# Layer-1 keys and experts: turned rows kept by token chunk, fifteen early weight loads, a ring of twelve, down two experts behind

## The reference

```python
x = layernorm(x + L0_attention(x))          # memory banks, 16 heads
x = layernorm(x + L0_experts(x))            # 16 routed experts, 2 shared ones
x = layernorm(x + L1_attention(x))          # linear attention with a feature map of two layers
x = layernorm(x + L1_experts(x))

# L1_experts: E = 64 experts, K = 6 of them for each token, H = 512, F = 192, CAP = 96
scores = sigmoid(x @ gate_w)
topk_ids = grouped_topk(scores + bias, K)                # best 4 of 8 groups first
topk_w = 2.5 * normalised(scores at topk_ids)
buf = first CAP tokens that chose each expert            # [64, 96, 512]
h = silu(buf @ w_gate) * (buf @ w_up)                    # [64, 96, 192]
out = h @ w_down                                         # [64, 96, 512]
y = segment_sum(out * topk_w, token)
shared = silu(x @ ws_gate) * (x @ ws_up) @ ws_down
return y + shared
```

## Time and profile before

| quantity | value |
| --- | --- |
| device time, three runs | median 1588.38 us (1587.12 to 1590.78) |
| the profiled execution's own time | 1585.73 us |
| its span | 1583.9 us |
| mean granted TensorE clock | 0.926 |
| TensorE busy | 1347.1 us, 85% of the span |
| VectorE busy | 1078.5 us, 68% |
| ScalarE busy | 730.1 us, 46% |
| GpSimd busy | 759.9 us, 48% |
| moved by DMA | 212.68 MB, mean 134 GB/s |

### The profile page before, as it was taken

How to read it: one execution, slowest core, us unless ns; L and a number is a source line. 1 busy time by engine, 2 the same in 40 slices (tenths; PEclk the granted TensorE clock), 3 DMA queues, 4 the chain that set the end, 5 groups by cost and what they waited for, 6 DMA issues and landing times. The chain is left out here.

```text
span 1583.9 us, 21495 instructions
## 1 busy us (share of the span) xinstructions
PE 1347.1 (85%) x7253; PEld 1110.7 (70%) x7253; DVE 1078.5 (68%) x1795; ACT 730.1 (46%) x1158; POOL 759.9 (48%) x654
## 2 busy tenths in 40 slices
PE   5999859999599999946999789998897799999950
PEld 5787647767377777735899679987666577777740
DVE  5688757232388888865886556666395588888847
ACT  4121032000188888832454354444221588888840
POOL 1455520000388887833664323332274467777734
PEclk9899979999799999977999789999997899999985
DMA  4000040000366567632110000002422999999958
GB/s 167 1 1 27 27 134 2 1 0 0 132 222 212 175 186 251 234 120 54 49 54 2 10 28 1 1 1 100 155 86 108 334 338 338 341 340 339 336 145 318
DMA packets 81808, 212.68 MB, mean 134 GB/s; under 512 B 20426, under 2 KB 23498, under 8 KB 79292
## 3 DMA queue, kind: packets, MB, share of 16 engines
q1 hardware_dynamic: 50075, 133.14, 23.2%
q0 software_dynamic: 31120, 77.38, 17.4%
q10 hardware_dynamic: 528, 1.05, 0.2%
HBM read 208.75 MB, written 46.79 MB: 161 GB/s over the span
## 5 line engine op out<-in xcount | busy, mean ns | idle before, releaser
L66 PE MATMUL bank<-e_w_hi,e_xt_hi 128*96 128x384 f32 (+1 forms) x444 | 168.4, 379 | 3.1 <-DVE e_w_lo L2700 3.1
L68 PE MATMUL bank<-e_w_hi,e_xt_lo 128*96 128x384 f32 (+1 forms) x444 | 160.8, 362 | 0.0
L67 PE MATMUL bank<-e_w_lo,e_xt_hi 128*96 128x384 f32 (+1 forms) x444 | 160.7, 362 | 0.0
L1064 POOL DMA_INDIRECT e_w_raw<-in_w_gate_up,r_load_of x47 | 54.6, 1161 | 215.5 <-issue 215.5
L2590 POOL DMA_INDIRECT sums<-e_y,r_target_of x64 | 108.4, 1694 | 73.1 <-DMA sums<-e_y,r_target_of 41.6
L1189 DVE TENSOR_TENSOR e_w_lo<-e_w_raw,e_w_hi 128x2048 fp32r<-128x2048 f32 x47 | 107.7, 2292 | 33.9 <-ACT e_w_hi L1148 26.3
L2700 DVE TENSOR_TENSOR e_w_lo<-r_w_early,e_w_hi 128x1536 fp32r<-128x1536 f32 x48 | 84.8, 1767 | 25.9 <-ACT e_w_hi L2664 24.9
L231 POOL TENSOR_TENSOR a_read<-a_read_n 128x256 f32<-128x256 f32 x64 | 50.2, 785 | 103.7 <-DVE a_read_n L452 103.7
L1056 POOL DMA_INDIRECT e_xg<-rows,r_token_of x47 | 91.5, 1947 | 14.3 <-issue 14.3
L1757 POOL TENSOR_TENSOR q_g_lo<-q_gf,a_g 128x512 fp32r<-128x512 f32 x32 | 41.6, 1301 | 112.2 <-ACT a_g L1921 112.2
L1148 ACT ACTIVATE e_w_hi<-e_w_raw 128x2048 fp32r<-128x2048 f32 x47 | 89.8, 1910 | 0.0
(11 more groups left out here) (481 smaller groups left out, 4463.2 us busy)
## 6 DMA issues: line engine op xcount, KB each, us to landing
r_w_early<-in_w_gate_up SPq DMA_DIRECT2D x48, 768.0 KB
r_w_early<-in_w_down SPq DMA_DIRECT2D x24, 768.0 KB
results<-e_y SPq DMA_DIRECT2D x47, 256.0 KB
rows<-resid SPq DMA_DIRECT2D x8, 1024.0 KB, 4.4
r_w_first<-in_w_gate_up SPq DMA_DIRECT2D x8, 768.0 KB
r_low<-in_w_down SPq DMA_DIRECT2D x8, 768.0 KB
e_w_raw<-in_w_gate_up SPq DMA_DIRECT2D x8, 768.0 KB
resid<-in_x SPq DMA_DIRECT2D x4, 1024.0 KB, 5.5
```

What stands on the lines that cost most here:

```text
L66: pe.matmul(out, a_hi, b_hi, start=start, stop=False)
L67: pe.matmul(out, a_hi, b_lo, start=False, stop=False)
L68: return pe.matmul(out, a_lo, b_hi, start=False, stop=stop)
L1064: pool.indirect_dma_start(w1_raw[p][:, :], None, io["w_gate_up0"], bass.IndirectOffsetOnAxis(k.load_of[:, c:c + 1], 0), bounds_check=E0 * ...
```

## The change

The turned rows of layer-1 attention now lie in one tile `xt` of [128, 4 chunks, 2 halves, 4, 512], high and low of one chunk side by side; `TurnedRows` gives the two views. Their chunks come free one after the other while the shared expert runs, and weights of the first ten routed experts are loaded into them and into the residual rows `k.x` as soon as these are stored: ten of gate and up, five pairs of down. Two gate-up loads and one down load start ahead of the zero stores; the rest follows `s_gu` at 2, 4 and 6 and the landing of the residual stores of a chunk. `s_sums0` becomes one semaphore for each chunk. GpSimd gathers for three experts before the block ends. The shared-expert block waits for what it waited for before.

In the routed block the ring has U = 12 buffers of gate and up weights and 6 of pairs of down weights, with loads ten experts ahead, and NR = 6 buffers of gathered rows with the gather of g+5. `pipeline` replaces `three_stages` on TensorE, ScalarE and VectorE: each stage is given with its distance from g, in the order in which it runs. `silu` and `hidden` are cut in two (`down_hi`, `down_lo` hold the down weights' part). `turn_hidden(g-1)` comes behind `gate_up(g)`, `down` and `results` are two experts behind, and `add_results` is that of g-2.

In `attention1_keys` the order of calls changes: `tile(0)` moves up ahead of `combine(5)`, `keys(2)` ahead of `normalise(2)`, and `combine(6)` and `turn(4)` are written out ahead of the loop.

The diff, shortened:

```diff
+def pipeline(eng, n, unroll, *stages):
+
+    def step(g):
+        for stage, ahead in stages:
+            if 0 <= g + ahead < n:
+                stage((g + ahead) // unroll, (g + ahead) % unroll)
+
+    first, last = -max(ahead for _, ahead in stages), -min(ahead for _, ahead in stages)
+    rounds = (n + first - 1) // unroll
+    for g in range(first, 2 * unroll + 1):
+        step(g)
+    with eng.Fori(2, rounds) as i:
+        for q in range(unroll):
+            for stage, ahead in stages:
+                stage(i + (q + 1 + ahead) // unroll, (q + 1 + ahead) % unroll)
+    for g in range(unroll * rounds + 1, n + last):
...
+class TurnedRows:
+
+    def __init__(self, both, half):
+        self.both, self.half = both, half
+
+    def __call__(self, b, first, n):
+        c, at = first // CH, first % CH
+        return self.both[:, c, self.half, b, at:at + n]
...
-        xt = tuple(k.sb("a1_xt_" + n, [P, KD, T], F32R, ctx) for n in ("hi", "lo"))
+        both = sb("xt", [P, NC, 2, KD, CH], F32R)
+        xt = tuple(TurnedRows(both, half) for half in range(2))
...
             combine(4)
+            tile(0)
             combine(5)
             rstd(2)
+            keys(2)
             normalise(2)
-            for i in range(NT):
+            combine(6)
+            turn(4)
+            for i in range(1, NT):
                 if i + 6 < NT:
                     combine(i + 6)
                     if i % 2:
@@ -1327,11 +1361,9 @@
                     keys(i + 2)
                 if i % 2 and i + 6 < NT:
                     normalise((i + 5) // 2)
-                if i:
-                    before_tile(i - 1)
+                before_tile(i - 1)
                 tile(i)
-                if i:
-                    after_tile(i - 1)
+                after_tile(i - 1)
             before_tile(NT - 1)
             after_tile(NT - 1)
...
-    k.s_sums0, k.s_sums1 = k.sem("e1_first_sums_begun"), k.sem("e1_second_sums_begun")
+    k.s_sums0, k.s_sums1 = [k.sem(f"e1_first_sums_begun{c}") for c in range(NC)], k.sem("e1_second_sums_begun")
...
-    k.xg_low = [low[0:CAP, 3 * D + n * (D + E1):3 * D + (n + 1) * (D + E1)] for n in range(2)]
+    row_at = lambda a, o: a[0:CAP, o:o + D + E1]
...
-    k.w1_early = [k.w1_first] + [rt(f"w1_early{p}", [P, KD, 2 * F1]) for p in range(1, 7)]
-    k.w2_early = [rt(f"w2_early{q}", [P, 3, D]) for q in range(3)]
-    k.xg_early = [rt(f"xg_early{p}", [CAP, D + E1]) for p in range(4)]
-    rt("early_rest", [P, 2 * KD * T - 9 * KD * 2 * F1 - 4 * (D + E1)])
-    k.s_w1_early = [k.sem(f"e1_gate_up_loaded{p}") for p in range(7)]
-    k.s_w2_early = [k.sem(f"e1_down_loaded{q}") for q in range(3)]
-    k.s_xg_early = [k.sem(f"e1_rows_gathered{p}") for p in range(4)]
+    freed = rt("early", [P, NC * 2 * KD * CH])
+    UNIT = KD * 2 * F1
+    unit = lambda n: freed[:, n * UNIT:(n + 1) * UNIT]
+    resid = lambda n: k.x[:, 3 * n:3 * n + 3, :].rearrange("p i d -> p (i d)")
+    gate_up_of = lambda a: a.rearrange("p (b n) -> p b n", b=KD)
+    down_of = lambda a: a.rearrange("p (f n) -> p f n", f=3)
+    k.w1_early = [k.w1_first[:, :, :]] + [gate_up_of(a) for a in (unit(1), unit(2), unit(3), unit(5), unit(6), unit(8), unit(9), resid(1), resid(2))]
+    k.w2_early = [down_of(a) for a in (unit(0), unit(4), unit(7), resid(0), resid(3))]
+    k.xg_early = [row_at(freed, 10 * UNIT), row_at(low, 3 * D), row_at(low, 3 * D + D + E1)]
...
+                gate_up_early(0)
+                down_early(0)
+                gate_up_early(1)
...
+                sp.wait_ge(s_gu, 2)
+                gate_up_early(2)
+                gate_up_early(3)
+                down_early(1)
+                sp.wait_ge(k.s_rows, 2 * 16 * NC)
+                store_rows(0)
+                store_rows(1)
                 sp.wait_ge(s_share, 1)
                 sp.dma_start(k.rows1.rearrange("(i p) d -> p i d", p=P)[:, :, D:D + E1], share[:, :, :]).then_inc(s_shared, 16)
-                sp.wait_ge(k.s_rows, 2 * 16 * NC)
-                for c in range(NC - 1):
-                    sp.wait_ge(s_res, TC * (c + 1))
-                    sp.dma_start(k.sums[0][0:T, :].rearrange("(c j p) d -> c p j d", p=P, j=TC)[c],
-                                 k.x[:, c * TC:(c + 1) * TC, :]).then_inc(k.s_sums0, 16)
+                sp.wait_ge(s_gu, 4)
+                gate_up_early(4)
+                gate_up_early(5)
+                down_early(2)
+                sp.wait_ge(k.s_sums0[0], 16)
+                down_early(3)
+                sp.wait_ge(k.s_sums0[1], 16)
+                gate_up_early(8)
+                store_rows(2)
                 sp.wait_ge(s_gu, NU - 2)
-                for e in range(6):
-                    if e:
-                        sp.dma_start(k.w1_early[e][:, :, :].rearrange("p b n -> p (b n)"), io["w_gate_up"][e]).then_inc(k.s_w1_early[e], 16)
-                    if e % 2 == 0:
-                        sp.dma_start(k.w2_early[e // 2][:, :, :].rearrange("p f n -> p (f n)"), io["w_down"][e // 2]).then_inc(k.s_w2_early[e // 2], 16)
+                gate_up_early(6)
+                gate_up_early(7)
+                sp.wait_ge(k.s_sums0[2], 16)
+                gate_up_early(9)
+                down_early(4)
...
-                for e in range(4):
-                    pool.indirect_dma_start(k.xg_early[e][:, :], None, k.rows1, bass.IndirectOffsetOnAxis(k.token_of[:, e:e + 1], 0)
+                for e in range(3):
+                    pool.indirect_dma_start(k.xg_early[e], None, k.rows1, bass.IndirectOffsetOnAxis(k.token_of[:, e:e + 1], 0)
...
-        U, NX = 8, 4
+        U, NX, NR = 12, 4, 6
...
-                    if not past(h, p, 6):
+                    if not past(h, p, 10):
...
-                three_stages(sp, E1, nothing, nothing, nothing, ahead=load, unroll=U, lead=6)
+                three_stages(sp, E1, nothing, nothing, nothing, ahead=load, unroll=U, lead=10)
...
-                    if past(h, p, U):
+                    if e >= NR:
...
                         pool.wait_ge(s_g[p], gathered(h, p) - 16)
-                        pool.wait_ge(s_wt, e - U + 1)
+                        pool.wait_ge(s_wt, e - NR + 1)
...
-                for g in range(-2, E1 + 1):
-                    if g + 6 < E1:
-                        gather((g + 6) // U, (g + 6) % U)
-                    if g == 1:
-                        pool.wait_ge(k.s_sums0, 16 * NC)
+                for g in range(-2, E1 + 2):
+                    if g + 5 < E1:
+                        gather((g + 5) // U, (g + 5) % U)
+                    if g == 2:
+                        for c in range(NC):
+                            pool.wait_ge(k.s_sums0[c], 16)
                         pool.wait_ge(k.s_sums1, 16 * (NC + 2))
-                    if g >= 1:
-                        add_results((g - 1) // U, (g - 1) % U)
+                    if g >= 2:
+                        add_results((g - 2) // U, (g - 2) % U)
...
-                three_stages(pe, E1, turn, gate_up, down, between=turn_hidden, unroll=U)
+                pipeline(pe, E1, U, (turn, 1), (gate_up, 0), (turn_hidden, -1), (down, -2))
...
-                three_stages(act, E1, turned_hi, silu, results, between=hidden_hi, prepare=weights_hi, unroll=U)
+                pipeline(act, E1, U, (turned_hi, 1), (weights_hi, 1), (silu, 0), (hidden_hi, -1), (down_hi, 0), (results, -2))
...
-                three_stages(vec, E1, turned_lo, hidden, nothing, between=hidden_lo, prepare=weights_lo, unroll=U)
+                pipeline(vec, E1, U, (turned_lo, 1), (weights_lo, 1), (hidden, 0), (hidden_lo, -1), (down_lo, 0))
```

More of the change, by code:

```diff
@@ L1482, in turn @@
                     act.wait_ge(s_tps, n + 1)
-                    act.activation(xt_hi[:, 2 * half:2 * half + 2, c * CK:(c + 1) * CK], bank[0][:, :].rearrange("p (b t) -> p b t", b=2),
+                    act.activation(xt_hi(slice(2 * half, 2 * half + 2), c * CK, CK), bank[0][:, :].rearrange("p (b t) -> p b t", b=2),
                                    ACT.Copy).then_inc(s_thi, 1)
@@ L1550, in turn @@
                     vec.wait_ge(s_thi, n + 1)
-                    part = lambda a: a[:, 2 * half:2 * half + 2, c * CK:(c + 1) * CK]
+                    part = lambda a: a(slice(2 * half, 2 * half + 2), c * CK, CK)
                     vec.tensor_tensor(part(xt_lo), bank[0][:, :].rearrange("p (b t) -> p b t", b=2), part(xt_hi), ALU.subtract).then_inc(s_tlo, 1)
@@ L2518, in experts1_routed @@
     with ExitStack() as ctx:
-        U, NX = 8, 4
+        U, NX, NR = 12, 4, 6
         two = lambda name, shape, dt=F32: [k.sb(f"e1_{name}{p}", shape, dt, ctx) for p in range(2)] * (U // 2)
         four = lambda name, shape, dt=F32: [k.sb(f"e1_{name}{p}", shape, dt, ctx) for p in range(NX)] * (U // NX)
-        w1_raw = k.w1_early + [k.sb(f"e1_w1_raw{p}", [P, KD, 2 * F1], F32, ctx) for p in range(7, U)]
+        w1_raw = k.w1_early + [k.sb(f"e1_w1_raw{p}", [P, KD, 2 * F1], F32, ctx)[:, :, :] for p in range(10, U)]
```

(14 more changed lines are left out.)

46 lines of the change are left out of this document (26 added, 20 removed).

## The result

Fourteen executions of each kernel: before 1586.92 us median (1584.69 to 1591.04), changed 1581.94 us (1575.05 to 1591.24). The ratio is 0.996 with a 95% interval of 0.9947 to 0.9974. The change is faster, by about 5 us instead of the 19 forecast, and the executions scatter over 16 us where those of before scattered over 6. The profiled execution of the changed kernel took 1575.05 us, span 1573.3: it is the fastest of the fourteen, and what its profile says of a step has to be read with that in mind. Of the 10.6 us between the two profiled spans, 2.7 lie ahead of layer-1 keys (694.47 before, 691.81 now), in work that the change doesn't touch.

A forecast was written before the change was run, and what follows sets the result against it. DMA and TensorE looked full in the routed stage, with TensorE's own 4.23 us left as the step. Terms -3.5 - 5.5 - 10.7 - 0.5 + 1.0 = -19.2 gave 1566.5 profiled, 1569 median; 8-in-10 range 1560 to 1584.

The forecast's parts named there:

- the order inside a step: Routed experts of layer 1: moving turn_hidden behind gate_up shortens a step from 4.456 to 4.28 us, -10.7 us over 61 steps.
- The first rival: Routed stage: additions to the sums set the step, holding it near 4.44 us; 1575 to 1579 us, chance 0.20.
- Boundary: Between shared-expert and routed blocks: fewer loads and gathers left to drain, so the next block starts earlier, -5.5 us.
- Loads ahead of the stage: Shared-expert block: eleven loads moved ahead of 1218, where DMA was 0.34 busy, cost 0 us.
- Keys: Layer-1 keys: tile(0) ahead of combine(5) fills TensorE's gap ahead of turn(4), -3.5 us.
- Fifteen loads as a head start: Routed weights: 34.8 us of transfers loaded ahead cover 27.5 us of falling behind at 4.28 a step; no starving.
- Tail: End of the routed stage: down one step further behind lengthens the last chain, +1.0 us.
- Clock: First step of the routed block: shorter pause leaves the granted clock nearer to full, -0.5 us.
- The slower rival: Routed stage: additions stay at their early pace of 4.85 us an expert throughout; near 1598 us, chance 0.06.

The follow-up runs named there:

- run 1: The changed kernel with the order of calls in layer-1 keys put back as before: 1582.66 us median.
- Runs 4: The changed kernel with twelve buffers of gathered rows instead of six and gathers nine steps ahead instead of five: 1578.83 us.
- 5: The kernel before with only the new order of the steps and additions two behind: 1589.57 us, ratio 1.0012 to the kernel before.
- run 10: The changed kernel with nine loads ahead of the routed stage and later loads six experts ahead instead of ten: 1583.61 us.
- run 3: The changed kernel with four sum tensors instead of two, half of the experts' results left out of the output: 1566.77 us.
- run 8: The changed kernel without the gathers from expert 6 on, later experts computing on the rows of the first six: 1558.39 us.
- 11: The changed kernel with eight result buffers, eleven of rows, eleven of gate and up weights, loops written out: 1572.27 us.

## Why the prediction was wrong

The step that failed is "the order inside a step": 61 x (4.456 - 4.28) = -10.7. The conversions of experts 2 and 63 stood 3.3 us closer than before in the fastest execution and 1.7 us further apart in a slow one. TensorE's step did become short, 4.10, even below what I took. What was mis-sized is the rate at which additions can follow. I had its row, 8.57 us for two between 1399.89 and 1408.46, and read it as 4.28 an expert, "just the step that I forecast". It was one of the shorter pairs. In the changed kernel 32 of the 34 additions of experts 12 to 45 are issued 0.3 us after the landing that they waited for, and the distance of two is 9.06 us in the mean, 9.41 in the profile of run 1: 4.5 to 4.7 an expert. In the kernel before the mean over the same experts was 8.85, which could have been read from its trace. But that is also twice its own step (2 x 4.456 = 8.91): there the results came no faster, so it says that the chain keeps up at 4.43 and not what it does beyond. The 20 waits of the earlier trace rows were the sign that little was left; how little, only the runs show.

The first rival, with a chance of 0.20, named this mechanism and gave 1575 to 1579; 1581.94 came. It had the hold end at ScalarE's `y`, and in the changed kernel it doesn't: no wait of ScalarE there is released by an addition. Runs 4 and 5, where the rows are asked for earlier, have such waits (16.7 and 22.8 us).

What the rival lacked is this: with six buffers and five steps of lead, TensorE runs out of gathered rows before ScalarE runs out of result buffers. I had counted only that gather and addition stay "seven apart as now". What matters is the time from a gather's issue to its use, which the lag of the additions eats. A gather stands in GpSimd's order right behind the addition of the expert eight before it. From that expert's result to the turn of the gathered rows were some 21 us before and are 15.5 now, since results come a step later and steps are shorter. With a lag of 5 us and more, 1.7 for GpSimd to get from the addition to the gather, and 8.5 for the landing nothing is left of that. Run 4 takes this wait away, and gives back 3 us.

By its other steps:

- Boundary, -5.5: the pause shrank by 6.2 us, by the mechanism named. The stage as a whole gained less, 2.0 to 2.4 us in eight of twelve profiles, and 5 to 6 in four.
- Loads ahead of the stage, 0: in those eight profiles the stage's work ended about 4 us later than before. Whether the loads have a part in it is open.
- Keys, -3.5: 2 to 3 us by the profiles, with TensorE's idle time down by 2.8.
- Fifteen loads as a head start that is needed: it isn't, at the rate of the additions (run 10). At 4.10 it would be, and falls short for some ten experts (run 3); my 34.8 us against 27.5 were reckoned for 4.28.
- Tail, +1.0: right. From the conversion of expert 63 to the last addition it is 13.10 us now and was 11.98. It is 13.0 to 13.2 in eight profiles with the new order, and 11.9 to 12.0 in the three with the old one.
- Clock, -0.5: from the block's first instruction on GpSimd to the conversion of expert 2 it took 10.04 us instead of 10.37, so 0.3 at most.
- The slower rival, additions at 4.85 throughout: not reached by the mean, though stretches of 5 us each exist. Its mechanism, VectorE and GpSimd keeping each other out, would have made GpSimd busier from 1300 to 1500; it was busy 135.96 us where it had been 147.29. It is not what makes the additions late: without loads they kept up at 4.15 with VectorE as dense (132.78 of 150 us busy). The 7.61 us of the earlier trace rows that it rested on were misnamed, too. L2217 is the product of silu and up, not a subtraction, and VectorE beside it compared and multiplied the tables of chosen experts.

In sum, keys, boundary and tail together explain 3 to 8 us, where 5 were gained in the median. The routed stage's steps gave 3.3 in the fastest execution and lost 1.7 in a slow one; what they give at the median is not shown.

## What to carry to other kernels

A chain in which each transfer waits for the landing of an earlier one has a rate of its own: read it as the mean distance over many pairs, under the traffic of that stage, before a faster step is counted in full. A mean taken where the chain only follows its producer shows no more than that it keeps up. If the chain is slower than the step, more buffers shift the moment at which it shows, one step's difference for each, and after that only more chains (here sum tensors) or lighter traffic help. When one engine issues both the chain and the loads that others need, a lag of the chain shortens the lead of those loads; compare what the lag leaves between a load's issue and its use with the landing time.

## What was not expected of the hardware

An indirect addition of 96 rows of 2 KB landed 4.2 us after its issue when weight loads were absent, and 8.5 us after it beside them, with the DMA engines moving 337 GB/s; the gathers went from 4.1 to between 8.1 and 8.5 us. How long the loads themselves took to land mattered little: with loads landing after 9 us (run 8, which has no gathers) the additions took 8.0, with 21 us 8.5, with 31 to 33 us (runs 3, 11) 9.0 to 9.4.
